# A four-layer graph network on one core: inverse roots on VectorE, counting by a summed tanh, and another order of stages in the messages' loop

## The reference, cut to what matters

```python
z = concatenate([x[src], x[dst], edge_attr]) @ W.T + b
msg = sigmoid(z) * where(z > 0, z, 0.01 * z)
x = layernorm(x + segment_sum(msg, dst, 50000))      # (x - mean) / sqrt(var + 1e-5)
```

## Time and profile before

| | |
|---|---|
| median of 3 runs | 3838.61 us (3825.87 to 3839.21) |
| profiled execution | 3831.48 us, span 3829.8 us |
| VectorE, ScalarE, GpSimd, PE busy | 60%, 55%, 53%, 49% of the span |
| mean granted TensorE clock | 0.734 |
| messages' loop | from about 34 us to about 1058 us |

### The profile page before, as it was taken

How to read it: one execution, slowest core, us unless ns; L and a number is a source line. 1 busy time by engine, 2 the same in 40 slices (tenths; PEclk the granted TensorE clock), 3 DMA queues, 4 the chain that set the end, 5 groups by cost and what they waited for, 6 DMA issues and landing times. The chain is left out here.

```text
span 3829.8 us, 53665 instructions
## 1 busy us (share of the span) xinstructions
PE 1871.1 (49%) x9516; PEld 1444.9 (38%) x9516; DVE 2305.8 (60%) x8726; ACT 2089.8 (55%) x5083; POOL 2039.4 (53%) x1895
## 2 busy tenths in 40 slices
PE   3333333333245454436777744544666566634443
PEld 2333333233233333324555422223555455523332
DVE  4443443443476666647788736664676677778884
ACT  2443343343343443427778847774444566649996
POOL 5445445445378888873333325554665555505554
PEclk8666666666667767768889979997888677755555
DMA  4444444444433343438999949885676667734442
GB/s 116 155 135 155 156 136 152 157 137 150 135 71 60 61 63 60 63 60 285 325 338 347 339 162 304 302 300 190 209 220 202 202 230 232 230 113 133 125 130 65
DMA packets 325290, 670.76 MB, mean 175 GB/s; under 512 B 56388, under 2 KB 115911, under 8 KB 325228
## 3 DMA queue, kind: packets, MB, share of 16 engines
q1 hardware_dynamic: 244716, 554.40, 42.8%
q0 software_dynamic: 80512, 115.76, 13.7%
HBM read 347.18 MB, written 326.96 MB: 176 GB/s over the span
## 5 line engine op out<-in xcount | busy, mean ns | idle before, releaser
L650 POOL DMA_INDIRECT src_rows<-x_table,row_i x400 | 407.6, 1019 | 376.0 <-PE ps L820 114.1
L1101 ACT ACTIVATE node_out<-node_in,n_shift,n_root 128x128 f32<-128x128 f32 (+1 forms) x1176 | 466.8, 483 | 0.4 <-DVE n_shift L1428 0.4
L1411 DVE BATCH_NORM_STATS2 n_stats<-node_in 128x6 f32<-128x256 f32 (+1 forms) x784 | 279.4, 419 | 294.0 <-DMA node_in<-in_x_dram 251.1
L872 PE MATMUL ps<-rise_hi,same_bf 125*128 125x201 bf16 x200 | 56.1, 308 | 646.6 <-DVE same_bf L1511 645.6
L726 POOL DMA_INDIRECT gat_sums<-sums,add_idx x200 | 328.8, 1644 | 68.0 <-issue 60.0
L1135 ACT ACTIVATE node_sums<-ps,srcb 128x201 f32<-128x201 f32 x200 | 74.6, 427 | 519.8 <-PE ps L873 519.7
L650 POOL DMA_INDIRECT sums<-gat_sums,dst_safe_i x200 | 189.6, 948 | 307.1 <-DVE pre L1688 249.2
L780 POOL DMA_INDIRECT out_dram<-new_rows,out_index x200 | 199.5, 997 | 249.6 <-ACT new_rows L1101 196.2
L650 POOL DMA_INDIRECT own_rows<-in_x_dram,dst_safe_i x200 | 190.4, 952 | 262.8 <-DVE pre L1497 216.5
L820 PE MATMUL ps<-ident,msg 128*128 128x128 f32 x602 | 120.2, 332 | 331.1 <-DVE msg L1734 173.5
L872 PEld LDWEIGHTS ps<-rise_hi,same_bf 125*128 125x128 bf16 x200 | 22.8, 114 | 660.7 <-issue 634.7
(11 more groups left out here) (328 smaller groups left out, 6904.7 us busy)
## 6 DMA issues: line engine op xcount, KB each, us to landing
own_rows<-x_table SPq DMA_DIRECT2D x300, 256.0 KB, 2.9
x_table<-node_out SPq DMA_DIRECT2D x144, 512.0 KB
acc_dump<-acc SPq DMA_DIRECT2D x200, 264.0 KB, 2.6
node_in<-x_table SPq DMA_DIRECT2D x96, 512.0 KB
x_table<-new_rows SPq DMA_DIRECT2D x150, 256.0 KB, 3.8
gat_sums<-node_x2t SPq DMA_DIRECT2D x49, 528.0 KB, 3.0
node_sums<-gat_sums SPq DMA_DIRECT2D x48, 528.0 KB
node_in<-in_x_dram SPq DMA_DIRECT2D x48, 512.0 KB
```

The lines of the kernel that those rows point to most:

```text
L650: g_.indirect_dma_start(out=to[:, g.b, j, 0:width], out_offset=None, in_=tab, in_offset=bass.IndirectOffsetOnAxis(ap=indices(j), axis=0)). ...
L872: te.matmul(ps[2][1][:, out_c], lhs, rise_hi[:, :], start=True, stop=False)
L1101: last = sc.activation(to[0:pn, g.b, j, :], rows[0:pn, g.b, j, 0:F], ACT.Identity, bias=NORM[k][2][0:pn, g.b, j:j + 1], scale=root[0:pn, j ...
L1411: last = v.bn_stats(NORM[k][0][0:pn, g.b, j:j + 2, :].rearrange("p j c -> p (j c)"), rows[0:pn, g.b, j:j + 2, 0:F].rearrange("p j f -> p f ...
```

## The change

The variances' inverse roots move from GpSimd to VectorE: a first guess by integer arithmetic on the bits, then three Newton steps, 11 instructions in all, each waiting for the one before. They stand between the node moments and the shifts, and the shifts' lags fall from 3 and 2 to 1 and 0. ScalarE's sigmoid becomes silu, so VectorE's product L1486 goes. The count becomes ScalarE's tanh(32 times the gap) with its sum taken by the same instruction; VectorE only copies eight sums a step away, and the index arithmetic after the loop grows from 15 instructions to 20. On SP the edge store gets lag 3 in place of 4 and stands ahead of the dump; the node store gets lag 2. ScalarE's edge norm gets lag 2 and stands behind silu, its node norm gets lag 1.

```diff
-            pipeline(sp, DENSE_FULL, edges((0, load_src_row), (0, load_ea), (1, dump), (4, store))
-                     + [nodes(1, zero_sums), nodes(3, store_nodes(D, x1_table, SLOTS)), nodes(0, load_nodes(D, x, 0, "n_row"))])
+            pipeline(sp, DENSE_FULL, edges((0, load_src_row), (0, load_ea), (3, store), (1, dump))
+                     + [nodes(1, zero_sums), nodes(2, store_nodes(D, x1_table, SLOTS)), nodes(0, load_nodes(D, x, 0, "n_row"))])
...
-            for s in range(STEPS + 2):
-                if s < STEPS:
-                    gather_ends(Step(s // 2, s % 2))
-                if 1 <= s:
-                    inverse_roots(s - 1)
+            unrolled(pool, (0, gather_ends))
...
-                sc.activation(gate[:, g.b, :, :].rearrange("p j f -> p (j f)"), ps[3][g.b][:, :], ACT.Sigmoid)\
+                sc.activation(gate[:, g.b, :, :].rearrange("p j f -> p (j f)"), ps[3][g.b][:, :], ACT.Silu)\
...
-                        last = sc.activation(gaps[:, g.b, 2 * h + i, :], ps[2][1][:, c], ACT.Relu, bias=one_of(srcb, g, 2 * h + i), scale=-1.0)
+                        sc.activation(gaps[:, g.b, j, 0:T], ps[2][1][:, at:at + T], ACT.Tanh, bias=one_of(srcb, g, j), scale=-STEEP,
+                                      accum_out=hit4[:, g.b, j:j + 1])
+                    sc.activation(hit4[:, g.b, J + 2 * h:J + 2 * h + 2], ps[2][1][:, T:2 * T + 2:T + 1], ACT.Copy).then_inc(L["dact"].sem, 1)
...
-            pipeline(act, DENSE_FULL, edges((0, gaps_of(0)), (3, new_x1), (1, sigmoid), (0, gaps_of(1)), (0, copy_ends)) + [nodes(2, new_nodes)])
+            pipeline(act, DENSE_FULL, edges((0, count_past(0)), (1, silu_messages), (2, new_x1), (0, count_past(1)), (0, copy_ends)) + [nodes(1, new_nodes)])
...
-                v.tensor_tensor(msg[:, g.b, :, 0:F], ps[3][g.b][:, :].rearrange("p (j f) -> p j f", f=F), gate[:, g.b, :, :], ALU.mult)
-                v.scalar_tensor_tensor(msg[:, g.b, :, 0:F], msg[:, g.b, :, 0:F], 0.01, msg[:, g.b, :, 0:F], ALU.mult, ALU.max)
+                v.scalar_tensor_tensor(msg[:, g.b, :, 0:F], gate[:, g.b, :, :], 0.01, gate[:, g.b, :, :], ALU.mult, ALU.max)
...
+            def inverse_roots(g, n=J + DJ):
+                def done(ins, i):
+                    ins.then_inc(N.sem, 1)
+                    wait_part(dve, N, g, i)
...
+                done(v.tensor_scalar(tmp.bitcast(i32), val.bitcast(i32), 1, None, ALU.logical_shift_right), 1)
+                done(v.tensor_scalar(y.bitcast(i32), tmp.bitcast(i32), -1.0, MAGIC, ALU.mult, ALU.add), 2)
+                for i in range(3):
+                    done(v.tensor_tensor(tmp, y, y, ALU.mult), 3 * i + 3)
+                    done(v.scalar_tensor_tensor(tmp2, tmp, -0.5, val, ALU.mult, ALU.mult), 3 * i + 4)
+                    done(v.scalar_tensor_tensor(y if i < 2 else val, tmp2, 1.5, y, ALU.add, ALU.mult), 3 * i + 5)
...
-            pipeline(dve, DENSE_FULL, edges((0, past_blocks), (3, x1_shifts)) + [nodes(2, node1_shifts)]
-                     + edges((1, message_sums), (1, x1_sums), (1, count_past)) + [nodes(0, node1_moments)])
+            pipeline(dve, DENSE_FULL, edges((0, past_blocks), (1, message_sums), (1, x1_sums), (1, keep_found)) + [nodes(0, node1_moments)]
+                     + [(0, inverse_roots, STEPS + 1)] + edges((1, x1_shifts)) + [nodes(0, node1_shifts)])
```

More of the change, by code:

```diff
@@ L47 @@
 LOW = 1e30
+STEEP = 32.0
+TIE = 11.0 / 128
+TIE_PART = 0.0040701
+HALF_UP = 1.5 * (1 << 23)
+MAGIC = 1597463007.0
 assert EP * T == N_EDGES and T % J == 0 and DENSE_FULL * P * DJ + TAIL_P * DJ == N_NODES
@@ L347, in gnn_program @@
         both_root = sb("both_root", [P, 2, J + DJ])
-        FIRST_NORM = {k: (NORM[k][0], both_root[:, :, c:c + n], NORM[k][2]) for k, c, n in (("e", 0, J), ("n", J, DJ))}
-        hit4 = sb("hit4", [P, 2, J])
+        newton = sb("newton", [P, 2, 3, J + DJ])
+        hit4 = sb("hit4", [P, 2, 2 * J])
         gaps = node_sums[:, :, :, :].rearrange("p b j f -> p (b j f)")[:, 0:2 * J * (T + 1)].rearrange("p (b j c) -> p b j c", b=2, j=J)
@@ L365, in gnn_program @@
         fix_ready, dummies_zero = sem("fix_ready"), sem("dummies_zero")
-        PER = {"accd": J, "spread": J, "dpe": 2, "dact": 2}
+        PER = {"accd": J, "spread": J, "dpe": 2, "dact": 2, "newton": 11}
         def norm(k, inverted=True):
@@ L1119, in copy_ends, with silu_messages, count_past @@
                 sc.activation(t_e[0:FE, g.b, :], ps[2][0][0:FE, :], ACT.Copy).then_inc(L["cp_e"].sem, 1)
-            def sigmoid(g):
+            def silu_messages(g):
                 wait_done(act, L["mm"], g)
-                wait_free(act, L["msg0"], g)
-                sc.activation(gate[:, g.b, :, :].rearrange("p j f -> p (j f)"), ps[3][g.b][:, :], ACT.Sigmoid)\
+                wait_free(act, L["msgd"], g)
+                sc.activation(gate[:, g.b, :, :].rearrange("p j f -> p (j f)"), ps[3][g.b][:, :], ACT.Silu)\
                     .then_inc(L["sig"].sem, 1)
-            def gaps_of(h):
+            def count_past(h):
                 def make(g):
@@ L1339, in _ @@
             link(v.tensor_tensor(block_hi[:, 0, :], block_hi[:, 0, :], block_hi[:, 1, :], ALU.subtract))
[L1340 to L1344, removed]
+            v.memset(rise_hi[:, :], 0.0)
+            v.memset(rise_lo[:, :], TIE)
+            link(v.memset(block_from[:, :], -1.0))
+            v.tensor_scalar(rise_hi[0:EP, 0:T], block_hi[:, 0, :], 256.0, None, ALU.mult)
+            v.tensor_tensor(rise_lo[0:EP, 0:T], block_lo[:, 0, :], block_lo[:, 1, :], ALU.subtract)
+            v.memset(rise_lo[0:EP, T:], 0.0)
+            v.memset(rise_hi[0:EP, T:], -float(T))
+            link(v.tensor_copy(block_from[0:EP, :], d[0:EP, 1:2]))
             v.memset(rise_hi[0:1, T:], 0.0)
@@ L1499, in x1_sums, with past_blocks @@
                 stats(L, "e", g, pre, P, jn)
-                variances(L, "e", g, P, jn, both_root[:, 1 - g.b, 0:J])
+                wait_done(dve, L["e_bn"], g)
+                v.tensor_scalar(both_root[:, 1 - g.b, 0:jn], NORM["e"][0][:, g.b, 0:jn, 2], 1.0 / F, EPS, ALU.mult, ALU.add).then_inc(L["e_ve"].sem, 1)
+            def past_blocks(g):
+                wait_landed(dve, L["srow_in"], g)
+                wait_free(dve, L["dpe"], g)
+                v.tensor_scalar(past[0:EP + 1, g.b, :], src_row[0:EP + 1, g.b, :], block_from[:, :], None, ALU.is_ge).then_inc(L["probe"].sem, 1)
@@ new lines, in keep_found, with node1_moments @@
+            def keep_found(g):
+                wait_done(dve, L["dact"], g)
+                v.tensor_copy(found_at[:, bass.ds(g.index() * (2 * J), 2 * J)], hit4[:, g.b, :]).then_inc(L["found"].sem, 1)
+            D = flow["nodes1"]
+            def node1_moments(g):
+                pn = dense_p(g)
+                wait_landed(dve, D["n_in"], g)
+                wait_free(dve, D["n_row"], g)
+                stats(D, "n", g, node_in, pn, DJ)
+                wait_done(dve, D["n_bn"], g)
+                v.tensor_scalar(both_root[0:pn, g.b, J:J + DJ], NORM["n"][0][0:pn, g.b, 0:DJ, 2], 1.0 / F, EPS, ALU.mult, ALU.add)\
+                    .then_inc(D["n_ve"].sem, 1)
@@ new lines, in inverse_roots @@
+            def inverse_roots(g, n=J + DJ):
+                N = L["newton"]
+                val, y, tmp, tmp2 = both_root[:, g.b, 0:n], newton[:, g.b, 0, 0:n], newton[:, g.b, 1, 0:n], newton[:, g.b, 2, 0:n]
+                def done(ins, i):
+                    ins.then_inc(N.sem, 1)
+                    wait_part(dve, N, g, i)
+                wait_previous(dve, L["e_ve"], g)
+                if not isinstance(g.k, int) or g.index() < DENSE_STEPS:
+                    wait_done(dve, D["n_ve"], g)
+                done(v.tensor_scalar(tmp.bitcast(i32), val.bitcast(i32), 1, None, ALU.logical_shift_right), 1)
[4 more added lines that the diff above has]
+                    done(v.scalar_tensor_tensor(y if i < 2 else val, tmp2, 1.5, y, ALU.add, ALU.mult), 3 * i + 5)
@@ L1506, in x1_shifts @@
                 shift_of(L, "e", g, P, jn, at)
[L1508 to L1528, removed]
             def node1_shifts(g):
-                dve.wait_ge(rt, g.index() + 1)
                 pn = dense_p(g)
@@ L1538, in _, with by_step @@
             fix_sums(L, F, 1)
             x1_sums(FIX, 1)
+            inverse_roots(Step(STEPS // 2, 1), 1)
             x1_shifts(FIX, 1)
             dve.wait_ge(L["found"].sem, L["found"].at(STEPS))
+            in_steps = found_at[:, :].rearrange("p (s c) -> p s c", c=2 * J)
+            def by_step(ap):
+                return ap.rearrange("p (s j) -> p s j", j=J)
+            link(v.tensor_scalar(by_step(hits[:, :]), in_steps[:, :, 0:J], 0.5, T / 2 + 0.002, ALU.mult, ALU.add))
             link(v.tensor_copy(w_i[:, :], hits[:, :]))
-            link(v.tensor_copy(w_a[:, :], w_i[:, :]))
@@ L1545, in _ @@
[L1545 to L1556, removed]
@@ L1557, in _ @@
-            v.tensor_copy(row_i[:, :], w_a[:, :]).then_inc(keyed, 1)
+            link(v.tensor_copy(w_a, w_i[:, :]))
```

(17 more changed lines are left out.)

38 lines of the change are left out of this document (11 added, 27 removed).

## The result

The kernel after takes **3966.85 us** (median; 3962.56 to 3972.13, 4 runs), the kernel before in the same session 3832.24 us (3819.51 to 3839.21, 4 runs). The ratio is **1.0356**, with a 95% interval of 1.032 to 1.0392: slower, as forecast, but by 135 us where 51 were forecast, and outside the range of 3850 to 3925 us. The profiled execution took 3962.79 us, its span is 3961.1 us, 131.3 us longer than that of before.

The account below looks back on a forecast made before the run. A ring of dependences passing twice through VectorE, 20.6 us, bounds each round. 2.7 - 0.7 - 1.0 + 0.1 = +1.1 us over 43 rounds is 47, plus 6 and 1.5: +55 us, forecast 3890 us, range 3850 to 3925.

Parts of the forecast that it names:

- The ring: Node rows, VectorE moments, PE, ScalarE's gate, VectorE sums, SP's load: a dependence cycle of 20.6 us that bounds each round.
- GpSimd's pace: GpSimd's power before the change: off the critical cycle, nothing waits for it, so removing it is worth nothing.
- ScalarE's summed tanh and copy: ScalarE: tanh with a sum and a small copy lie in its 10 us wait and cost nothing.
- The Newton steps: VectorE, node moments to PE's probes: 13 links of 0.2 us plus 0.12, +2.7 us a round (bounds 2.2 to 3.3).
- The product: VectorE, gate to sums: L1486 and its link leave, -0.7 us a round; silu stays at 0.60 us.
- the term for SP's order: SP: edge store's 256 KB leave the burst ahead of the node rows, -1.0 us a round (bounds 0.8 to 1.4).
- the +0.1 for a gather: GpSimd, without its power, starts the x[src] gathers about when node rows land: +0.1 us a round (bounds 0 to 1.2).
- the third rival: GpSimd, free of its wait, puts the whole x[src] gather into the burst: +1.1 us a round, 3942 us, chance 0.08.
- the one on tables: ScalarE: silu and tanh in different tables, silu's 1.28 us load exposed each round, 3954 us; chance 0.04.
- The early step of the earlier trace: Early step without the edge store: VectorE starts 7.2 us after the sums against 8.4, used for the upper bound 1.4.
- The rest of the sum: Outside the 43 rounds: four first rounds some +1.6 each, 6 us; after the loop +1.5 us.
- The load's gain paying for the roots: SP's node load lands 6.3 us behind the sums, cancelling the round's cost: no slower, 3840 us; chance 0.14.

Follow-up runs that it names:

- e1: Kernel after, with GpSimd waiting again for the node moments as its power did before; 3963.84 us, ratio 1.0342 to the kernel before.
- e4: Kernel after with both the edits of e1 and e3; 3827.18 us, ratio 0.9976 to the kernel before.
- e3: Kernel after with the roots a round later, in VectorE's wait for the node rows; 3828.23 us, ratio 0.9974 to the kernel before.
- f1: Kernel after with the edge store behind the dump and the gather of x[dst] held back; 3906.68 us, ratio 1.017 to the kernel before.
- e5: Kernel after with the gather of x[dst] held until the node moments of the step before; 4135.51 us, ratio 1.0469 to the kernel before.
- b1: Kernel before with only SP's edge store moved ahead of the dump; 3956.23 us, ratio 1.0013 to the kernel before.
- e6: Kernel after with the node load ahead of edge store and dump on SP; 3838.16 us, ratio 0.9728 to the kernel before.
- f3: Kernel after with dump, zeros and both stores a round later on SP, source line ahead of the dump; 3640.64 us, ratio 0.9475 to the kernel before.
- e2: Kernel after with the edge store back behind the dump; 3939.06 us, ratio 1.0286 to the kernel before.

## Why the prediction was right or wrong

**What bounds the kernel: right.** The ring through both waits of VectorE is the kernel's: its pieces add up to the round in both kernels. GpSimd's pace, off the ring, was worth nothing (e1, e4), and the roots on it came back in full (e3). ScalarE's summed tanh and copy were not tested by themselves; they run in its wait for PE, which is still 11.2 us a round (190.7 us in 17 waits).

**The Newton steps: right.** 2.7 us forecast from a link of 0.2 us, +2.82 measured in the piece, and e3 gives it back. An instruction lasts 0.17 us, and it is 0.205 us from start to start. The Trainium skill's 58 cycles and a column each ("VectorE: DVE Perf Modes", section on the TRN2 errata), which the prediction set against this, give 0.07 us and don't hold at this size. The same section says below its table that this row comes out too short and that the fixed term measured is about 150 cycles; for twelve columns that is 0.17 us (an estimate), and the trace agrees. The prediction left that sentence out.

**The product: right.** -0.7 forecast, -0.77 measured, silu as long as the sigmoid (0.60 us).

**The wrong step is the term for SP's order**, "I take 1.0, as the engines are busy all through", together with the +0.1 for a gather. The two should have brought -0.9 us and brought +0.52, a miss of 1.4 us a round or 61 us over 43 rounds. The earlier issue was right (-0.61). What failed is the treatment of the burst as a sum of bytes from which 256 KB can be struck. The term has its sign and about its size where no gather is in the burst (0.68 us in f1 against e5; its bounds were 0.8 to 1.4), and it has the other sign beside the gather. And the gather that collides is not the one the third rival named: not `x[src]` set free by the missing power (e1, e4), but `x[dst]`, which starts 1.3 us behind the dump in both kernels. The figures of that rival and of the one on tables, 3942 and 3954 us, were nearer to the result than the forecast, and the cause of neither was at work. The early step of the earlier trace rows misled: a landing at 7.2 us without the store was read as the store's worth. That step has a gather in its burst too, but its packets are not slow. From 4 to 7 us behind its dump, in the kernel before:

```profile
q0 software_dynamic: 35, 0.08, 10.8%
```

That is 0.15 us a packet. With the store moved and not left out, it is 0.57.

**PE at +0.26 us: not forecast, and its cause stays open.** The granted clock came back later. The fifth microsecond of the probes and products in before, then in after (length, busy times of PE, PEld, DVE, ACT, POOL, then PEclk, DMA share, GB/s):

```profile
423.40:424.40 1.00, 1.00 (x9) 1.00 (x9) 0.00 (x0) 0.00 (x0) 0.93 (x1) 0.81 0.26 66
```

```profile
524.05:525.05 1.00, 1.00 (x7) 1.00 (x7) 0.00 (x0) 0.00 (x0) 0.00 (x0) 0.50 0.00 0
```

0.50 is 1.2 GHz; in before a part of that microsecond ran at 2.4. Both rows have PE fully busy. One would put it down to PE standing idle longer ahead of its probe (15.99 us in the round shown, 13.58 in the earlier trace rows), but the other runs speak against that. In e3 PE was idle for 12.9 us on average, less than in before (13.4), and the piece is 5.69 us; in b1, with 13.9 us, it is 5.07. What does go with the piece is when the clock rises: on average 3.8 us behind the first probe in b1, 4.5 in before, 5.0 in after, 5.2 in e3. Over 43 rounds the 0.26 us are 11 us.

**The rest of the sum.** The fifth start of the node moments lies 8.9 us later than in before (6 forecast), the last regular one, at 1121.64 against 990.21, 131.4 later, so the 43 rounds between cost 122.5, 2.85 each. The last instruction of the row indices starts at 1194.17 against 1057.91, 136.3 later: 4.9 us for the last rounds, the extra step and the index work, where 1.5 were forecast. Behind it 5 us come back to the span's 131.3; where wasn't looked into, and executions of one kernel differ by more than that (3819.51 to 3839.21 us).

**The other rivals.** Tables: the trace of after has no table load in the loop, silu and tanh alternate without one. The load's gain paying for the roots: the landing would have had to come at 6.3 us, it came at 8.85.

## What to carry to other kernels

Where a few transfers decide a round, ask which of them must land first and how many bytes and gathers lie ahead of it: putting the load ahead of the burst was worth 6% here (after to e6) and the source line with it a further 2.5% (e6 to f3), while taking another transfer from ahead of it made it 0.6% slower (e2 to e1). These steps compare ratios, the first two across sets. A dependent chain of small instructions cost its links (0.2 us each) on the ring, and nothing in a wait on the same engine (e3); so look first for a wait to put it into, and check that what ends this wait isn't behind the chain. Two transfers that share a burst are not two terms of a sum: the store's effect changed sign with the gather, and only the four-cell table showed it.

## What the runs showed of the hardware

A packet of the gather, of 2 to 3 KB, took 0.10 us on its engine in before and 0.44 us in b1, where only the place of a third transfer had changed (means over the rounds, from 4 to 7 us behind the dump). On ScalarE an instruction with a sum is followed by one that reads it out, 0.19 us for each tanh of 0.41 us. The roots' integer steps (a shift, and a multiply and add on int32) last as long as float ones, 0.17 us for 12 columns. And TensorE's granted clock rose 3.8 us behind the first probe in one kernel (b1) and 5.2 us in another (e3) with rounds of nearly the same length, which changed PE's piece by 0.6 us.
